# Long cross attention by pairs of heads: 64-row tiles for the scores, full banks of transposes, one run of value products a pair

## The reference, cut to what matters

```python
def _L2_xattn_ref(Q, K, V, mask, Wq, bq, Wk, bk, Wv, bv, Wo, bo):
    ...
    q = _split_heads(Q @ Wq.T + bq)
    k = _split_heads(K @ Wk.T + bk)
    v = _split_heads(V @ Wv.T + bv)
    scores = jnp.einsum('bhqd,bhkd->bhqk', q, k) * scale
    scores = jnp.where(mask == 0, jnp.asarray(-jnp.inf, scores.dtype), scores)
    attn = jax.nn.softmax(scores, axis=-1)
    out = jnp.einsum('bhqk,bhkd->bhqd', attn, v)
    ...
    return out @ Wo.T + bo
```

## Time and profile before

| | |
|---|---|
| three runs | 1897.12, 1902.21 and 1908.44 us; median 1902.21 |
| profiled execution | 1898.67 us, of it the span of the trace 1896.9 us |
| busy: PE, PEld, DVE, ACT | 1634.8, 1243.8, 1069.8, 897.2 us |
| L2x | scores from 437 us, next layer at about 1022 us |
| L3x | first key copies at 1154 us, last scores at 1749 us |
| TensorE clock, mean over the span | 0.934 of full |

### The profile page before, as it was taken

One profiled execution on the slowest core, in us unless ns is written; L12 is line 12 of the kernel. 1 busy time (PEld: TensorE's weight loads), 2 busy tenths in 40 slices (PEclk: granted clock), 3 DMA queues, 4 the chain that ended last, 5 costly groups with the idle time before them and its releaser, 6 DMA issues.

```text
span 1896.9 us, 34030 instructions
## 1 busy us (share of the span) xinstructions
PE 1634.8 (86%) x13482; PEld 1243.8 (66%) x13482; DVE 1069.8 (56%) x1958; ACT 897.2 (47%) x1439; POOL 15.1 (1%) x23
## 2 busy tenths in 40 slices
PE   0597896467999999999997797799999999999499
PEld 0365484335878787777885465687787878788355
DVE  6422323455677667767685326576767767677312
ACT  0020130003676667666775122566667666668221
POOL 0000000100000000000000000000000000000000
PEclk9798998678999999999998798899999999999599
DMA  8466664137354647445332265646545454630354
GB/s 341 125 181 214 222 174 166 40 110 175 80 136 98 152 98 162 98 118 137 79 79 90 73 254 138 158 98 147 129 88 137 98 141 98 157 79 17 133 215 186
DMA packets 42810, 257.09 MB, mean 136 GB/s; under 512 B 9928, under 2 KB 10184, under 8 KB 33992
## 3 DMA queue, kind: packets, MB, share of 16 engines
q1 hardware_dynamic: 42664, 255.05, 48.6%
HBM read 152.12 MB, written 0.13 MB: 80 GB/s over the span
## 4 chain that ended last, share of the span: by engine, by line
PE 68%; DMA 11%; SPq 9%; DVE 7%; ACT 2%; issue 2%; POOL 1%; POOLq 0%; DVEq 0%; ACTq 0%
PE T L534 13%; SPq L450 9%; PE O L635 9%; PE S L611 7%; PE S L539 7%; DMA keys<-keys_hl 6%; PE O L534 5%; PE T L586 5%; PE O L697 4%; PE T L599 4%; PE O L586 3%; PE S L814 2%; DMA ctx_in<-in_ctx_cols 2%; PE O L599 2%; PE O L847 2%
## 5 line engine op out<-in xcount | busy, mean ns | idle before, releaser
L1224 DVE CUSTOM_DVE_ANT_0 sc<-S,mask_bias,small 128x896 f32<-128x896 f32 x448 | 513.6, 1146 | 183.8 <-PE S L611 182.7
L926 ACT ACTIVATE sc<-sc,small 128x1792 f32<-128x1792 f32 x224 | 399.9, 1785 | 0.0
L534 PE MATMUL T<-consts,sc 128*128 128x128 f32 (+1 forms) x2204 | 340.4, 278 | 25.6 <-DVE keys_hl L1167 9.3
L534 PEld LDWEIGHTS T<-consts,sc 128*128 128x128 f32 (+1 forms) x2204 | 262.7, 141 | 103.3 <-issue 46.8
L912 ACT ACTIVATE pT<-T 128x512 f32<-128x512 f32 x448 | 231.5, 522 | 160.8 <-PE T L534 160.8
L611 PE MATMUL S<-keys,q 128*128 128x512 f32 (+1 forms) x896 | 294.4, 410 | 1.4 <-DMA keys<-keys_hl 1.4
L635 PE MATMUL O<-pT,arena 128*32 128x128 f32 x6272 | 238.8, 276 | 0.0
L635 PEld LDWEIGHTS O<-pT,arena 128*32 128x32 f32 x6272 | 179.1, 109 | 37.3 <-issue 37.2
L534 PE MATMUL O<-consts,sc 128*128 128x128 f32 x1044 | 167.9, 278 | 26.1 <-DVE keys_hl L1167 13.2
L534 PEld LDWEIGHTS O<-consts,sc 128*128 128x128 f32 x1044 | 125.0, 141 | 62.9 <-issue 23.0
L912 ACT ACTIVATE pT<-O 128x512 f32<-128x512 f32 (+1 forms) x224 | 117.2, 523 | 81.2 <-PE O L534 81.2
(11 more groups left out here) (281 smaller groups left out, 1456.2 us busy)
## 6 DMA issues: line engine op xcount, KB each, us to landing
keys<-keys_hl SPq DMA_DIRECT2D x448, 224.0 KB, 5.8
ctx_in<-in_ctx_cols SPq DMA_DIRECT2D x42, 896.0 KB, 7.3
wide<-in_up_L3f SPq DMA_DIRECT2D x8, 2048.0 KB, 9.0
wide<-in_ctx_rows SPq DMA_DIRECT2D x14, 896.0 KB, 5.5
wide<-in_up_L0f SPq DMA_DIRECT2D x8, 1408.0 KB, 9.3
sc<-in_ctx_cols SPq DMA_DIRECT2D x10, 896.0 KB, 7.9
wide<-in_up_L2f SPq DMA_DIRECT2D x8, 1024.0 KB, 6.7
wide<-in_down_L2f SPq DMA_DIRECT2D x8, 1024.0 KB, 4.8
```

What stands on the lines that cost most here:

```text
L534: last = nc.tensor.transpose(out[0:w, t * P:(t + 1) * P], src[:, t * w:(t + 1) * w], ident)
L926: nc.scalar.activation(sc[:, n % 3, :], sc[:, n % 3, :], ACT.Exp, bias=n_best[c % 2][:, h:h + 1], scale=-1.0, accum_out=l_new[c % 2][:, h: ...
L1224: V.tensor_tensor_reduce(sc[:, n % 3, i * HC:(i + 1) * HC], S4f[:, i * 2 * BANK:i * 2 * BANK + HC], mask_bias[:, i * HC:(i + 1) * HC], 1.0 ...
```

## The change

A pair of heads becomes the unit of work in L2x and L3x; a cross layer has 56 pair steps m = 8c + j.

- **Scores.** `q4` holds each head's queries in 64 rows of its own (upper, upper, rest, rest of its 16 dimensions), and `keys4` the keys to match, both heads of a pair one under the other. A score matmul contracts over 64 rows instead of 128; the two heads' matmuls are issued alternately into different banks, and both heads have their two halves in turn in the same banks. The zeros are gone.
- **Key copies.** `load_keys` issues, for a half of the keys, 32 transfers of 16 partitions (row length 1792 as before) in place of 16 transfers of 32.
- **Transposes.** The 28 blocks of a pair fill seven whole banks; the bank in the middle has blocks of both heads. VectorE copies groups 0 and 6, ScalarE 1 to 5.
- **Value products.** One run of 28 blocks a pair, at the end of the same step. `pT2` now holds one pair, so the next pair's copies wait for that run.
- **Projections.** New places: the keys' first half in pairs 1 to 3, their second half in pairs 5 to 7.
- `sc` gets a fourth buffer in a part of `packs1`.

```diff
-HEADS_ALL = NC * H
+PAIRS = NC * NP
 KEY_UNITS = CH // (HC // 2)
 VALUE_UNITS = TB // 2
-
-PROJECTED = {2: [("K", 0, 0)], 3: [("K", 0, 1)], 4: [("K", 0, 2)], 5: [("K", 0, 3)],
-             6: [("V", 0)], 7: [("V", 1)], 8: [("V", 2)], 9: [("V", 3)], 10: [("V", 4)],
-             11: [("K", 1, 0)], 12: [("K", 1, 1)], 13: [("K", 1, 2)], 14: [("K", 1, 3)],
-             15: [("V", 5), ("V", 6)]}
-
-
-def projected(n):
-
-    c, h = divmod(n, H)
...
+TURNS = 2 * TB // 4
+HR = P // 2
+KEY_COPIES = 4 * H // 2
+
+PROJECTED = {0: [("V", 0), ("V", 1)], 1: [("K", 0, 0), ("V", 2)], 2: [("K", 0, 1), ("K", 0, 2)],
+             3: [("K", 0, 3), ("V", 3)], 4: [("V", 4), ("V", 5)], 5: [("K", 1, 0), ("V", 6)],
+             6: [("K", 1, 1), ("K", 1, 2)], 7: [("K", 1, 3)]}
+
+
+def projected(m, i):
+
+    c, j = divmod(m, NP)
+    if c + 1 >= NC or i >= len(PROJECTED[j]):
+        return None
+    u = PROJECTED[j][i]
+    return (u[0], c + 1, *u[1:])
...
-            units += [("T", n, g) for g in range(3)] + projected(n) + [("T", n, 3)]
+    for m in range(PAIRS):
+        units += [("T", m, g) for g in range(3)] + [projected(m, 0), ("T", m, 3)]
+        if quad_turned(m) is not None:
+            units.append(("O", quad_turned(m)))
+        units += [("T", m, g) for g in range(4, TURNS)] + [projected(m, 1)]
...
-    return "act" if u[0] == "T" and u[2] != 1 else "dve"
+    return "act" if u[0] == "T" and u[2] not in (0, TURNS - 1) else "dve"
...
-        q4 = nc.alloc_sbuf_tensor_at("q4", [P, H, P], F32R, offset=packs1_at + 4 * spare)
+        q4 = nc.alloc_sbuf_tensor_at("q4", [P, NP, P], F32R, offset=work_at + 4 * BANK)
+        sc_last = packs[1][:, packs1_used:packs1_used + CH]
+
+        def weights_of(n):
+
+            return sc[:, n % 4, :] if n % 4 < 3 else sc_last
...
-                            sp.wait_ge(s["s_ready"], 2 * (H * (c - 1) + HH * (hf + 1)))
-                        for r in range(4):
-                            for j in range(HH // 2):
-                                sp.dma_start(keys4[QR * r:QR * (r + 1), hf * HH // 2 + j, :].bitcast(F32),
-                                             keys_hl[QR * j:QR * (j + 1), r % 2, :].bitcast(F32)) \
-                                    .then_inc(s[f"keys_in{hf}"], 16)
+                            sp.wait_ge(s["s_ready"], 2 * (NP * (c - 1) + NP // 2 * (hf + 1)))
+                        for j in range(HH // 2):
+                            for a2 in range(2):
+                                for r in range(4):
+                                    sp.dma_start(keys4[HR * a2 + DH * r:HR * a2 + DH * (r + 1),
+                                                       hf * HH // 2 + j, :].bitcast(F32),
+                                                 keys_hl[QR * j + DH * a2:QR * j + DH * (a2 + 1), r % 2, :].bitcast(F32)) \
+                                        .then_inc(s[f"keys_in{hf}"], 16)
 
                     def load_next_ctx(c, half):
 
                         if c + 1 >= NC:
                             return
-                        if c == 0:
-                            last = "K", 0, 1, 2 * half + 1
-                        else:
-                            last = ("V", c, VALUE_UNITS - 1) if half else ("K", c, 1, 1)
-                        sp.wait_ge(s["t_ready"], UNIT_AT[last] + 1)
+                        sp.wait_ge(s["t_ready"], UNIT_AT["K", c, 1, 2 * half + 1] + 1)
...
-                def scores(n, half):
-
-                    c, h = divmod(n, H)
-                    if h % HH == 0 and half == 0:
-                        pe.wait_ge(s[f"keys_in{h // HH}"], 16 * 16 * (c + 1))
-                    if n:
-                        pe.wait_ge(s["s_taken"], 2 * (n - 1) + half + 1)
+                def scores(m, half):
+
+                    c, j = divmod(m, NP)
+                    if half == 0 and j % (NP // 2) == 0:
+                        pe.wait_ge(s[f"keys_in{j // (NP // 2)}"], KEY_COPIES * 16 * (c + 1))
+                    if m or half:
+
+                        pe.wait_ge(s["s_taken"], 4 * m + 2 * half)
                     for n0, n1 in ((0, BANK), (BANK, HC)):
-                        last = mm(S4f[:, half * 2 * BANK + n0:half * 2 * BANK + n1], q4[:, h, :],
-                                  keys4[:, h // 2, half * HC + n0:half * HC + n1], start=True, stop=True)
+                        for i in range(2):
+                            own = slice(HR * i, HR * (i + 1))
+                            last = mm(S4f[:, i * 2 * BANK + n0:i * 2 * BANK + n1], q4[own, j, :],
+                                      keys4[own, j, half * HC + n0:half * HC + n1], start=True, stop=True)
                     last.then_inc(s["s_ready"], 1)
 
-                def turn(n, g):
-
-                    u = ("T", n, g)
+                def turn(m, g):
+
+                    u = ("T", m, g)
                     if g == 0:
-                        pe.wait_ge(s["p_ready"], n + 1)
+                        pe.wait_ge(s["p_ready"], 2 * m + 1)
+                    if 4 * g < TB <= 4 * g + 3:
+                        pe.wait_ge(s["p_ready"], 2 * m + 2)
                     bank_free(u)
-                    blocks = min(4, TB - 4 * g)
-                    transposes(ring(u), sc[:, n % 3, 4 * g * P:(4 * g + blocks) * P], blocks).then_inc(s["t_ready"], 1)
-
-                def multiply(n):
-
-                    c, h = divmod(n, H)
-                    if h == 0:
+                    for t in range(4):
+                        i, b = divmod(4 * g + t, TB)
+                        last = nc.tensor.transpose(ring(u)[:, t * P:(t + 1) * P],
+                                                   weights_of(2 * m + i)[:, b * P:(b + 1) * P], ident)
+                    last.then_inc(s["t_ready"], 1)
...
-                    for b in range(TB):
-                        i = b % 4
-                        last = mm(O2[32 * i:32 * i + 32, 1, (h % 4) * P:(h % 4 + 1) * P],
-                                  vv[:, c % 2, b, (h // 2) * 32:(h // 2 + 1) * 32],
-                                  pT2[:, (n % 2) * CH + b * P:(n % 2) * CH + (b + 1) * P],
-                                  start=(b < 4), stop=(b >= TB - 4))
+                    if m % 2 == 0 and m:
+                        pe.wait_ge(s["o_taken"], m // 2)
+                    pe.wait_ge(s["t_dve"], emptied(("T", m, TURNS - 1)))
+                    pe.wait_ge(s["t_act"], emptied(("T", m, TURNS - 2)))
+                    for t in range(2 * TB):
+                        i, b = divmod(t, TB)
+                        g = t % 4
+                        at = (2 * (m % 2) + i) * P
+                        last = mm(O2[32 * g:32 * g + 32, 1, at:at + P], vv[:, c % 2, b, j * 32:(j + 1) * 32],
+                                  pT2[:, t * P:(t + 1) * P], start=(b < 4), stop=(b >= TB - 4))
...
-                for n in range(HEADS_ALL + 2):
-                    if n < HEADS_ALL:
-                        turn(n, 0)
-                        if n + 2 < HEADS_ALL:
-                            scores(n + 2, 0)
-                        turn(n, 1)
-                        turn(n, 2)
-                        if n + 2 < HEADS_ALL:
-                            scores(n + 2, 1)
-                        for u in projected(n):
-                            (key_unit if u[0] == "K" else value_unit)(*u[1:])
-                        turn(n, 3)
-                    if 0 < n <= HEADS_ALL:
-                        multiply(n - 1)
-                    if quad_turned(n) is not None:
-                        turn_quad(quad_turned(n))
...
+                for m in range(PAIRS):
+                    turn(m, 0)
+                    turn(m, 1)
+                    if m + 1 < PAIRS:
+                        scores(m + 1, 0)
+                    turn(m, 2)
+                    project(m, 0)
+                    turn(m, 3)
+                    if quad_turned(m) is not None:
+                        turn_quad(quad_turned(m))
+                    if m + 1 < PAIRS:
+                        scores(m + 1, 1)
+                    for g in range(4, TURNS):
+                        turn(m, g)
+                    project(m, 1)
+                    multiply(m)
+                turn_quad(PAIRS // 2 - 1)
...
-                        act.wait_ge(s["keys_in0"], 16 * 16 * (c + 1))
+                        act.wait_ge(s["keys_in0"], KEY_COPIES * 16 * (c + 1))
                     elif nb == 0 and c:
-                        act.wait_ge(s["keys_in1"], 16 * 16 * c)
+                        act.wait_ge(s["keys_in1"], KEY_COPIES * 16 * c)
...
+                for m in range(PAIRS):
+                    if quad_turned(m) is not None:
+                        take_quad(quad_turned(m))
+                    take_turned(m, 1)
+                    take_turned(m, 2)
+                    project(m, 0)
+                    take_turned(m, 3)
+                    take_turned(m, 4)
+                    take_turned(m, 5)
+                    if m + 1 < PAIRS:
+                        soften(2 * m + 2)
```

(18 more changed lines are left out.)

172 lines of the change are left out of this document (71 added, 101 removed).

## The result

The changed kernel takes 2229.99 us (median of 4 runs, 2229.53 to 2235.98) beside 1902.34 us of the kernel before (4 runs, 1897.12 to 1908.44): 1.1728 times as long, 95% interval 1.1688 to 1.1769. The direction was forecast, the size not: 2405 us lay 175 us too high, and the range began at 2280. The profiled execution has a span of 2228.3 us, 331.4 more than before.

The account below looks back on a forecast made before the run. The prediction took the loop of key-copy batch and following phase, with TensorE waiting for the batch, as the bound. 1898.7 us plus 436 (second to fourteenth batches), 36 (first batches) and 34 (tails) gave 2405 us, range 2280 to 2465.

Parts of the forecast that it names:

- each of the 32 costs what one of the 16 did: Key copies: a transfer of 16 partitions takes as long as one of 32, about 1.15 us, one after another.
- Batch of key copies: SyncE's copies for half of the keys: 2.9 + 31 x 1.15 = 38.5 us, from 20.7 before.
- Phase: From last key copy landed to next batch: two pairs, a value unit, three key units, slow clock; 22.1 us.
- Second to fourteenth batch: Twelve batches with phases a layer at 60.7 us each, 728 us; 436 us more over both layers.
- First batches: TensorE waiting for each layer's first key copies before its first scores: 18 us more a layer, 36 in all.
- After the fourteenth batch: Each layer's last eight pairs, paced by VectorE: 12 us more, plus 5 us waiting for the batch; 34 for two layers.
- TensorE's work in a pair: Transposes 2.77, products 1.95, scores 1.72, outputs 0.2: 6.6 us a pair against 7.1 before.
- the rival of 2452 us: Score tiles not side by side, with the long batch: 0.98 us more a pair, 2452 us; chance 0.14.
- issue pace: Rival: SyncE's issue at 0.84 us a transfer sets the batch, 29.5 us, giving 2161 us; chance 0.07.
- A batch of 20.7 us with 16 partitions: Rival: 16 rows take half the time of 32, so batches stay short; 1885 us or 1850; chance 0.08.
- The rival that new waits eat what a pair saves: With short batches, new waits cancel the 0.5 us saved a pair: within 0.5%, 1893 to 1912 us; chance 0.03.
- The likeliest case: Long key batches with score tiles side by side: 2405 us, its own range 2340 to 2455; chance 0.68.

Follow-up runs that it names:

- Experiment 6: The changed kernel with all 32 transfers of a batch reading partitions 0 to 15 of keys_hl: 2434.84 us.
- experiment 4: The changed kernel with the 16 key copies of each pair's second head issued by GpSimd instead of SyncE: 2180.33 us.
- the order runs: The changed kernel with its 32 copies reordered: neighbours on different partitions at both ends, 2092.06 us; four on end into one destination, 2306.94 us.
- experiments 5 and 9: 5: changed kernel with the earlier 16 copies of 32 partitions, 1916.41 us; 9: changed kernel with key units in two places and neighbouring copies on different partitions, 1911.46 us.
- experiment 1: The kernel before with only its key copies cut into 32 transfers of 16 partitions: 1999.74 us, 1.0510 times before.

## Why the prediction was wrong in size

The mechanism was right: fewer partitions, longer batches, TensorE waiting for them once a half. The step that failed is the term "each of the 32 costs what one of the 16 did", and with it a batch of 38.5 us. The signs that the prediction named came out the same way, each short of its number: ScalarE's wait 14.7 us on average where 16 to 19 were named, a chunk of 109.7 us with TensorE busy for 74% where 120 and 65% were, 123 GB/s where 100 were.

- **Batch of key copies.** 38.5 said, 31.6 measured. Experiment 6 gives 38.7 where no source changes, so the price of a single transfer stood; wrong was that transfers stand one behind another whatever they touch. "All read the same few partitions, four transfers on end" was written, and what happens at the fifth was not asked. In 24 phases this is 24 x 6.9 = 166 us too much. What sets the price where neighbours differ is shown only as far as the orders tried: 26.2, 31.6, 33.8 and 38.7 us.
- **Phase.** 22.1 said, 22.95 measured, +20 us in 24. The clock's 2.0 us was right: from 983.80 to 988.64, behind the wait, two banks of transposes and a value unit take 4.84 us, four of them at a granted clock of 0.50, where the same stretch from 961.66, at full clock, takes 2.84. The work is 0.85 more than I counted, 0.2 of it in the two pairs.
- **Second to fourteenth batch**, both layers: 436 said, 144.2 + 145.6 = 290 measured; the two points above make up the difference, -166 + 20.
- **First batches.** 36 said. To the first scores it was 11.8 + 11.6 = 23.4: the same term, 2 x 6.9 less. From there to the second batch another 3.4 + 2.3 = 5.7 us were added that the sum had at nothing.
- **After the fourteenth batch.** 34 said, 13.2 measured. The walk through a pair held: 8.66 us from scores to scores, with the two waits it named:

```profile
1154.77 0.68 PE L618 MATMUL S<-keys,q 64*128 64x512 f32 x4
...
1157.77 0.68 PE L618 MATMUL S<-keys,q 64*128 64x512 f32 x4 [0.87 <-DVE small L1247]
...
1160.74 1.74 PE L649 MATMUL O<-pT,arena 128*32 128x128 f32 x56 [0.83 <-DVE pT L1213]
...
1163.43 0.68 PE L618 MATMUL S<-keys,q 64*128 64x512 f32 x4
```

  The eight pairs of the last chunk, from the products ahead of them to their last products, take 67.5 us against 56.7 before, +10.8 (12 said; the last pair is short). But 3.8 us less lie ahead of them: before, two value units and the rest of two heads come behind the fourteenth batch, now they don't. I had not looked at what else stands there. And the stall of 5 us was 0.8, the batch being shorter.
- **TensorE's work in a pair.** 6.6 said, 6.7 measured with the same share of the outputs. The parts were off by more than the sum: a score run costs 0.61 plus what its neighbours lose, about 0.75, against 0.86, while a bank of transposes takes 0.44 (961.66 to 962.10) against 0.395, 0.3 us more in seven banks. That the sum came close is in part luck. That the tiles work side by side held, so the rival of 2452 us fell.

Sum: 290 + 23.4 + 5.7 + 13.2 = 332 against 331.4 in the spans; the rest lies outside the two layers.

Of the other rivals, issue pace fell with experiment 4 and the order runs, where the same number of transfers is issued in 22.9 us. Its number, a batch of 29.5 and 2161 us, would have been the nearer one, for a wrong reason. A batch of 20.7 us with 16 partitions showed in no order tried; the shortest was 26.2. Nor did SyncE by itself ever issue that fast: the rival's condition was 0.56 us an issue, and 32 issues took at least 21.4 us in every run here, 0.67 each. The rival that new waits eat what a pair saves is what experiments 5 and 9 show once the batches are short or covered. The range ended at 2280, which is a batch of 34 us (38.5 - 125/28); between the bounds of the batch, 20.7 and 38.5, stood no case but the one on issue, though nothing in the rows excluded the middle. The likeliest case's own upper end doesn't follow from its terms: 28 batches by 1.6 us and 24 phases by 1.5 are 81 us above 2405, not 50; the miss was on the other side.

## What to carry to other kernels

In the orders tried here the full price of 1.14 us a transfer was paid only where all read the same partitions: ask what the next one touches before multiplying, and try the order of transfers, at both ends, before their number. Ahead of that, ask what covers a batch: moving the producers together, so that about three and a half pairs instead of two lie between batches, gave back 294 of 328 us with the slow copies still in place. And when a new order only pays in work saved, look for single waits taken for a whole tile where each piece could be waited for; here that alone turned 0.25% into 1.8%.

## What the runs showed of the hardware that was not expected

- The same 32 copies of 112 KB within SBUF take 38.7 us with one source, 33.8 with four on end to one destination, 31.6 with four on end from one source and changing destinations, 26.2 with both ends changing.
- SyncE's issues of such copies come 0.67 us apart on average at the fastest (21.4 us for 32 with half the bytes, 21.5 with all of them in experiment 1), and stretch when transfers back up: 34.7 us for 32 with one source. An issue interval is thus no sign of an issue limit.
- Two 64-row tiles of scores gain the same whether the matmuls alternate or not (1910.63 and 1911.46 us; 0.61 us a run in both). A run for one head in its tile takes 0.60 us, a run for both heads 0.61, and a run for one head over 128 rows took 0.49.
